# Two graph layers in one kernel: layer 2 with the adjacency as weights, and four smaller moves in layer 1

## The reference

```
h  = relu(layernorm(x))
s  = (h @ W) @ a1 ;  t = (V @ W) @ a2
e  = leaky(s[:, None] + t[None, :], 0.2), where adj > 0, else -9e15
x  = x + elu(softmax(e, axis=1) @ V + h)
h2 = relu(layernorm(x))
x  = x + relu((adj.T @ h2) @ U.T / adj.sum(axis=0)[:, None])
```

## Time and profile before

| | us |
|---|---|
| median of 3 runs (lowest, highest) | 490.03 (489.5, 490.09) |
| the profiled execution | 489.36 |
| its span | 487.5 |
| PE / DVE / ACT / POOL busy | 425.2 / 299.1 / 255.0 / 127.8 |
| weight row copied on ACT (L448), starts | 11.63 |
| last quarter of V landed (issued 5.47, under way 9.13) | 14.6 |
| first adjacency load issued; lands after | 15.26; 7.7 |
| third and fourth adjacency load: issued; land after | 16.5 and 17.0; 16.2 and 20.5 |
| first guard; shifts of group 0 turned (1.87); seeds; first mask | 26.23; 46.71; 49.26; 50.08 |
| closing of group 4: DVE starts at 407.00, h2 scaled at 416.69 + 0.69 | 10.4 |
| one score of 5 blocks on DVE (L738) | 0.86 |
| relu and exp of 5 blocks on ACT: 109.18 (0.77), 110.10 (0.79) | 1.6 |
| DVE step over 256 elements (L875, L878) | 0.40 to 0.42 |
| ACT copy of 500 columns from PSUM; POOL's subtraction (L379) | 0.59; 1.15 |
| clock granted to TensorE, mean share | 0.963 |

### The profile page before, as it was taken

How to read it: one execution, slowest core, us unless ns; L and a number is a source line. 1 busy time by engine, 2 the same in 40 slices (tenths; PEclk the granted TensorE clock), 3 DMA queues, 4 the chain that set the end, 5 groups by cost and what they waited for, 6 DMA issues and landing times.

```text
span 487.5 us, 9207 instructions
## 1 busy us (share of the span) xinstructions
PE 425.2 (87%) x3966; PEld 200.5 (41%) x3966; DVE 299.1 (61%) x401; ACT 255.0 (52%) x306; POOL 127.8 (26%) x118
## 2 busy tenths in 40 slices
PE   0511989799987999998999999999999999999996
PEld 0411344354332544332444333354333436655563
DVE  4799489669999578999469999523443313101011
ACT  1210457575654776776776766877777741100010
POOL 8750058476242702321202223101010001200000
PEclk9975699799999999999999999999999999999999
DMA  9799999999999790000000000000000000000001
GB/s 162 83 107 108 107 102 107 108 107 109 107 102 101 77 99 1 1 2 0 1 1 2 1 1 1 1 1 1 1 1 2 1 1 3 0 12 12 21 19 27
DMA packets 17638, 20.74 MB, mean 43 GB/s; under 512 B 13409, under 2 KB 13473, under 8 KB 17598
## 3 DMA queue, kind: packets, MB, share of 16 engines
q0 software_dynamic: 4752, 16.90, 33.5%
q1 hardware_dynamic: 8606, 2.18, 2.3%
q10 hardware_dynamic: 4240, 1.08, 1.3%
HBM read 69.79 MB, written 1.05 MB: 145 GB/s over the span
## 4 chain that ended last, share of the span: by engine, by line
PE 60%; DVE 23%; issue 9%; ACT 4%; DMA 2%; ACTq 1%; POOL 1%; DVEq 0%; POOLq 0%
PE att L988 16%; DVE junk L692 14%; PE q L972 10%; PE den L991 9%; PE q L1077 7%; DVE arena L738 5%; PE q L1047 3%; PE den L1077 3%; DMA v_sb<-n_L_gnn_entity_embs_dram 2%; PE att L1077 2%; PE z L937 2%; ACT q L529 2%; PE z L952 2%; ACT arena L513 2%; PE z L1093 1%
## 5 line engine op out<-in xcount | busy, mean ns | idle before, releaser
L988 PE MATMUL att<-arena,v_sb 128*64 128x500 f32 (+2 forms) x640 | 151.1, 541 | 5.0 <-ACT arena L517 3.2
L692 DVE CUSTOM_DVE_ANT_0 junk<-adj_sb,t_row 125x2048 uint8<-125x2048 uint8 x66 | 153.5, 2326 | 0.7
L738 DVE SCALAR_TENSOR_TENSOR arena<-arena,b_col,q 128x1000 f32<-128x1000 f32 (+2 forms) x80 | 85.7, 1071 | 89.5 <-PE q L972 89.5
L517 ACT ACTIVATE arena<-arena,t 128x1000 f32<-128x1000 f32 (+2 forms) x80 | 78.6, 982 | 89.0 <-DVE arena L738 88.9
L972 PE MATMUL q<-bi,adj_sb 128*128 128x125 bf16 (+1 forms) x1088 | 90.1, 221 | 14.7 <-ACT q L529 9.8
L991 PE MATMUL den<-arena,ones 128*32 128x250 f32 (+1 forms) x1280 | 94.5, 354 | 0.0
L972 PEld LDWEIGHTS q<-bi,adj_sb 128*128 128x128 fp8e4 x1088 | 64.4, 99 | 72.1 <-issue 42.9
L529 ACT ACTIVATE q<-arena,minus_b 128x1000 f32<-128x1000 f32 (+2 forms) x80 | 76.0, 950 | 7.3 <-PE q L963 1.2
L513 ACT ACTIVATE arena<-q,t_col 128x1000 f32<-128x1000 f32 (+2 forms) x80 | 74.7, 934 | 2.8 <-PE q L972 2.4
L991 PEld LDWEIGHTS den<-arena,ones 128*32 128x32 f32 x1280 | 25.4, 109 | 107.9 <-issue 107.9
L988 PEld LDWEIGHTS att<-arena,v_sb 128*64 128x64 f32 x640 | 32.2, 137 | 22.8 <-ACT arena L517 5.6
(11 more groups left out here) (152 smaller groups left out, 295.6 us busy)
## 6 DMA issues: line engine op xcount, KB each, us to landing
adj_sb<-in_adj_dram POOLq DMA_DIRECT2D x33, 500.0 KB, 28.6
v_sb<-n_L_gnn_entity_embs_dram ACTq DMA_DIRECT2D x4, 256.0 KB, 9.1
x_sb<-in_x_dram SPq DMA_DIRECT2D x1, 928.0 KB
out_dram<-x_sb SPq DMA_DIRECT2D x7, 124.0 KB
x_sb<-in_x_dram SPq DMA_DIRECT2D x1, 125.0 KB
out_dram<-x_sb SPq DMA_DIRECT2D x1, 125.0 KB
buf_a<-in_L_gnn_a_dram ACTq DMA_DIRECT2D x1, 32.0 KB, 3.0
buf_b<-in_L_gnn_U_dram SPq DMA_DIRECT2D x2, 16.0 KB, 6.4
```

Of the source, the lines that this page charges most:

```text
L517: nc.scalar.activation(e_part(n % E_SLOTS, nb), e_part(n % E_SLOTS, nb), ACT.Exp, bias=t02[:, c:c + 1])\
L692: nc.vector.tensor_tensor_reduce(out=junk[0:R, :], in0=adj_bytes[0:R, b, half], in1=t_row[0:R, half], scale=1.0 / ONE, scalar=0.0, op0=ALU ...
L738: nc.vector.scalar_tensor_tensor(out=e_part(n % E_SLOTS, nb), in0=a_part(nb), scalar=b_col[:, c:c + 1], in1=part(q[0], nb), op0=ALU.max, o ...
L988: nc.tensor.matmul(att[h * D:(h + 1) * D, 0:(k1 - k0) * R], v_sb[:, c, :], e[:, k0 * R:k1 * R], start=first, stop=final)
```

## The change

1. **Layer 2** takes the adjacency as weights: for each of the 33 blocks of output rows, 33 matmuls with 129 moving columns (h2 high, h2 low, a column of ones whose sum is the degree). The twelve outputs `OUTS` have three or two blocks, one PSUM bank each. Counts, degrees, the copies of the sums and the products go away. U moves into each closing: PE turns h2 (`turn_h2`, tile 17), ACT copies (`copy_turned`, 18), PE multiplies by a doubled U (`times_u`, 19), ACT makes two copies (`high`, 20). U's rows are scaled to norm 1 and the norm is multiplied back at the end (`u_scale`).
2. **Leaky parts**: DVE takes 12, 6, 12, 12, 20 tiles of the five groups, ACT the others; the tiles 0 and 1 of a group are always DVE's. Either kind may use either `q`; the seeds go.
3. **V** comes by two queues, two quarters each; on SP's they stand before x. Five blocks get their ones before V is weighed, and the adjacency loads no longer wait for x.
4. **The mean of V** stands in front of the tiles, behind six of group 0's eight guards.
5. **Turns in bf16**: the shifts are turned in bf16, and turns of fp32 data are transposes.

```diff
-    ONES_FIRST = 9
+    ONES_FIRST = 5
-    ON_ACT = [c % 2 == 1 for i, c in TILES]
-    FIRST_ON_ACT = ON_ACT.index(True)
-    CHUNKS = [(4 * i, 4 * i + 4) for i in range(7)] + [(28, 29), (29, 33)]
+    ON_DVE = (12, 6, 12, 12, 20)
+    ON_ACT = [c >= 2 and (c - 1) * (ON_DVE[i] - 2) // (NC - 2) == (c - 2) * (ON_DVE[i] - 2) // (NC - 2) for i, c in TILES]
+    OUTS = [(3 * i, 3 * i + 3) for i in range(9)] + [(27, 29), (29, 31), (31, 33)]
+    PART_A = 6
+    STORE = 112
...
-        turn = sb("turn", [P, 8, 32])
+        turn = sb("turn", [P, 8, 32], bf16)
...
+        TURN_H2, COPY_H2, TIMES_U, HIGH = 17, 18, 19, 20
...
+            def load_v(i):
+                chunks = slice(i * NC // PARTS, (i + 1) * NC // PARTS)
+                sp.dma_start(v_sb[:, chunks, :], v_view[:, chunks, :]).then_inc(v_in[i], 16)
+
             sp.dma_start(w_sb, W[:, :]).then_inc(wa_in, 16)
+            load_v(1)
+            load_v(3)
             sp.dma_start(x_sb[:, 0:SHORT, :], x_short).then_inc(x_in, 16)
...
+                sp.wait_ge(fin_done, o + 1)
+                sp.dma_start(to[0:STORE], x_sb[0:STORE, b0:b1, :]).then_inc(out_stored, 16)
+                sp.dma_start(to[STORE:rows], x_sb[STORE:rows, b0:b1, :]).then_inc(out_stored, 16)
...
-            pool.wait_ge(x_in, 32)
             for b in range(ONES_FIRST):
                 load(b)
+            for b in range(ONES_FIRST, 7):
+                set_ones(b)
+                load(b)
...
+            nc.gpsimd.memset(h2[:, :, 2 * D:2 * D + 1], 1.0).then_inc(ones_made, 1)
+            pool.wait_ge(u_bounded, 1)
+            pool.wait_ge(ones_made, 1)
+            nc.gpsimd.tensor_tensor(u_inverse[:, :], u_squares[:, :], minus_half[0:D, 0:1], ALU.pow).then_inc(u_inverted, 1)
...
-            for i in range(PARTS):
+            for i in (0, 2):
                 chunks = slice(i * NC // PARTS, (i + 1) * NC // PARTS)
                 act.dma_start(v_sb[:, chunks, :], v_view[:, chunks, :]).then_inc(v_in[i], 16)
...
-                act.wait_ge(h2_done, i + 1)
-                nc.scalar.activation(h2[0:R, b0:b1, 0:D], buf_a[0:R, 0:b1 - b0, :], ACT.Copy).then_inc(hi_done, 1)
+                act.wait_ge(h2_multiplied, i + 1)
+                nc.scalar.activation(h2[0:R, b0:b1, 0:D], product, ACT.Copy).then_inc(hi_done, 1)
+                nc.scalar.activation(buf_a[0:R, 0:b1 - b0, :], product, ACT.Copy).then_inc(h2_copied, 1)
...
+            for o, (b0, b1) in enumerate(OUTS):
+                rows, nb = rows_of(b0), b1 - b0
+                mine = buf_a[0:rows, o % 2 * 4:o % 2 * 4 + nb, :]
+                dve.wait_ge(gathered, o + 1)
...
+                nc.vector.reciprocal(rdeg[0:rows, 0:nb].unsqueeze(2), sums(o)[:, :, 2 * D:2 * D + 1]).then_inc(rdeg_done, 1)
...
+                nc.vector.tensor_reduce(mine, sums(o)[:, :, 0:2 * D].rearrange("p k (h d) -> p k d h", h=2), AX.X, ALU.add)\
+                    .then_inc(halves_added, 1)
...
+                nc.vector.scalar_tensor_tensor(out=mine, in0=mine, scalar=0.0, in1=rdeg[0:rows, 0:nb].unsqueeze(2).to_broadcast([rows, nb, D]),
+                                               op0=ALU.max, op1=ALU.mult).then_inc(scaled, 1)
...
+                nc.vector.tensor_tensor(mine, mine, u_scale[0:rows, :].unsqueeze(1).to_broadcast([rows, nb, D]), ALU.mult)\
+                    .then_inc(widened, 1)
...
+                nc.vector.tensor_tensor(x_sb[0:rows, b0:b1, :], x_sb[0:rows, b0:b1, :], mine, ALU.add).then_inc(fin_done, 1)
...
-                    pe.wait_ge(a_copied, 1)
-                    pe.wait_ge(bi_made, 1)
+                    pe.wait_ge(guarded, 2 * GROUPS[0][1] - 2)
                 last = nc.tensor.matmul(z[:, 1, :], mean_w, v_sb[:, 8 * k:8 * k + 8, :].rearrange("p c d -> p (c d)"),
...
-                    nc.tensor.matmul(z[0:R, 0, k * P:(k + 1) * P], scratch[:, k * R:(k + 1) * R], ident[:, :], start=True, stop=True)
+                    turn_over(z[0:R, 0, k * P:(k + 1) * P], scratch[:, k * R:(k + 1) * R], P)
...
             rows(0)
+            for k in range(4):
+                mean_v(k)
             turn_shifts(0)
...
+            def gather(o, first, last_one):
...
+                for k in range(b1 - b0):
+                    start = first_row(b0 + k)
+                    for b in range(first, last_one):
+                        rows = rows_of(b)
+                        done = nc.tensor.matmul(out_bank(o)[0:out_rows, k * (2 * D + 1):(k + 1) * (2 * D + 1)],
+                                                adj_sb[0:rows, b, start:start + out_rows], h2[0:rows, b, 0:2 * D + 1],
+                                                start=(b == 0 and k == 0), stop=(b == NB - 1 and k == b1 - b0 - 1))
...
+            late = GROUPS[-1][0]
+            pe.wait_ge(exped, len(TILES))
+            pe.wait_ge(lo_done, NI - 1)
+            pe.wait_ge(ones_made, 1)
+            gather(0, 0, late)
             to_natural(NI - 1)
...
+            for o in (1, 2, 3):
+                gather(o, 0, late)
+            turn_h2(NI - 1)
+            gather(4, 0, late)
+            times_u(NI - 1)
+            gather(5, 0, late)
+            pe.wait_ge(lo_done, NI)
+            for o in range(PART_A):
+                gather(o, late, NB)
+            for o in range(PART_A, len(OUTS)):
+                gather(o, 0, NB)
```

More of the change, by code:

```diff
@@ L542, in _ @@
                         square2(i - 1)
+                    if c == COPY_H2:
+                        copy_turned(i - 1)
                     if c == HIGH:
@@ L563, in _ @@
             copy_att(NI - 1)
[L565 to L570 removed]
             act.wait_ge(weighed, NC * NI)
[L573 removed]
             exp_hp(NI - 1)
             square2(NI - 1)
+            copy_turned(NI - 1)
             high(NI - 1)
[L577 to L583 removed]
         @block.vector
@@ L936, in turn_shifts @@
                     for bank, start, c0, c1 in block_parts(nb, k):
-                        last = nc.tensor.matmul(z[96:P, bank, start:start + c1 - c0], turn[0:R, k, :], ident[0:R, c0:c1],
+                        last = nc.tensor.matmul(z[96:P, bank, start:start + c1 - c0], turn[0:R, k, :], ident16[0:R, c0:c1],
                                                 start=True, stop=True)
@@ L1027, in _ @@
                     to_natural(i - 1)
+                if i >= 1 and c == TURN_H2:
+                    turn_h2(i - 1)
+                if i >= 1 and c == TIMES_U:
+                    times_u(i - 1)
                 if i == 0:
-                    if MEAN_V <= c < MEAN_V + 4:
-                        mean_v(c - MEAN_V)
                     if c == TURN_U:
@@ L1039, in _ @@
                 attend(n, *TILES[n])
-            def count(k):
-                pe.wait_ge(exped, len(TILES))
-                for b in range(NB):
-                    for quarter, n in enumerate(COUNTS[k]):
-                        first = first_row(CHUNKS[n][0])
-                        last = nc.tensor.matmul(count_banks[k][32 * quarter:32 * quarter + 32, 0:width(n)], ones16[0:rows_of(b), :],
-                                                adj_sb[0:rows_of(b), b, first:first + width(n)], start=(b == 0), stop=(b == NB - 1))
-                last.then_inc(counted, 1)
@@ L1064, in gather @@
-            def gather(n):
-                first = first_row(CHUNKS[n][0])
-                if n in (3, 4, 5):
-                    pe.wait_ge(deg_copied, n - 2)
-                if n >= 6:
-                    pe.wait_ge(agg_copied, n - 5)
-                for b in range(NB):
-                    if n == 0 and b == 0:
-                        pe.wait_ge(lo_done, NI - 1)
-                    if n == 0 and b == GROUPS[-1][0]:
-                        pe.wait_ge(lo_done, NI)
-                    rows = rows_of(b)
-                    last = nc.tensor.matmul(gather_banks[n % 6][:, 0:width(n)], h2[0:rows, b, :],
-                                            adj_sb[0:rows, b, first:first + width(n)], start=(b == 0), stop=(b == NB - 1))
-                last.then_inc(gathered, 1)
```

247 lines of the change are left out of this document (122 added, 125 removed).

## The result

The changed kernel takes **483.18 us** (median of 11 runs, 481.83 to 488.35) against 489.36 for the one before (11 runs, 488.64 to 490.24): a ratio of 0.9887, 95% interval 0.9857 to 0.9917. It is faster, by 6 us where 45 were forecast, and lies above the range of 434 to 470. The profiled execution took 482.21, its span is 480.4.

A forecast was written before the change was run, and what follows sets the result against it. PE was taken to bound groups 2 to 4 and layer 2, with waits in groups 0 to 3. Terms -6.5 - 9.9 - 5.1 - 2.7 - 2.2 + 1.0 - 19.9 = -45.3 gave 445 us, range 434 to 470.

The forecast's parts named there:

- The tiles: Groups 0 to 4: new DVE/ACT sharing shrinks waits; terms -9.9, -5.1, -2.7, -2.2 and +1.0 us.
- PE's floors: Groups 1 to 3: PE's time with no wait after the change, put at 59.4, 72.6 and 72.6 us.
- Rival (c): Groups 0 to 3: new sharing moves the wait to ACT, they gain half or nothing; 455 to 465 us, 13%.
- the closing of group 4 hides: Layer 2's beginning: gathers cover the last group's closing chain; if that failed, a wait of 1 to 2 us.
- Group 0: First group's tiles: loses mean of V and seeds, PE and DVE level at 42; 47 us, -9.9.
- Group 4: Last group's tiles: no turn of shifts to save on, h2 turn and U added; +1.0 us.
- Layer 2: Final gather: 1089 matmuls with adjacency as weights, 66.0 us against 85.9, -19.9.
- The open price: Layer 2: cost of the weight load behind each matmul, taken as 57 ns, ends 56.4 and 111.
- (a): Layer 2: load costs more than the matmul, 65 to 84 ns instead of 57; 454 to 474 us, 14%.
- (b): Layer 2: load goes at fp32's rate, 111 ns a pair, 59 us more; 504 us, 9%.
- The start: Before the first mask: V by two queues -4.5 us, seeds and half the turn -2.0; first mask near 43.5.
- rival (d): Start: two queues don't bring V sooner, or x is caught among large transfers; +5 to +10, 450 to 455 us, 7%.

The follow-up runs named there:

- the best kernel: The changed kernel with the old sharing (every odd tile on ACT) and DVE's sums of s at tile 24 instead of 21: 453.41 us, 0.9271.
- the alternation: The changed kernel with the old sharing of the leaky parts back, every odd tile on ACT, 16 and 16: 461.3 us, 0.9444.
- the moved guards: Guards dealt over the first 23 tiles instead of 26, against the 453.4 us kernel with old alternation and sums at tile 24: 463.55 us, 0.9472.

## Why the prediction failed, point by point

**The failed step** is the one called "The tiles", at the sentence "I expect DVE's waits to shrink, not to go", and with it the terms -5.1, -2.7 and -2.2 of groups 1 to 3. These terms left 2, 1.4 and 1.4 us of waits above PE's floors of 59.4, 72.6 and 72.6; measured above the floors are 8.7, 11.5 and 14.6. The step compared each engine's sum with the stage (ACT 66 of 73, DVE 49 of 60) and took the difference as slack. The sums were not far off: ACT has 59.9 in group 2, DVE 49.35 in group 1. What decides is which wait stands ahead of which instruction in an in-order queue, and that I did not write out for the new rule. Had I laid tiles 0 to 5 of a group in a row, relu 2 behind exp 0, relu 3 and the copy of att behind exp 1 were plain to see, with two guards in front. Those first tiles are where the whole price of the sharing sits, some 19 us over the five groups. The floors were also reckoned at full clock; behind the waits it was half.

**Rival (c)** had the same places and the right sign against the forecast, with the wrong mechanism (ACT's load, 2.27 against 2.12) and the wrong size: "gain half or nothing". A sharing that couples engines can lose, and did, 15 us in the kernel before.

**The second oversight** is the late product. In the closing I counted what the product adds on PE and asked whether the closing of group 4 hides; for groups 0 to 3 I followed the closing to `high` but not to who waits behind it: POOL's low half, `weigh_h` behind that, `sum_s` at tile 21. "What is late next" was the question to ask of every tile number moved from 17 to 20. It cost 7.9 to 13.2 us.

**Group 0** was put at 47 with ends of 43 and 54; it took 52.8, and 50.8 in the best kernel. The premise, two engines level at 42, did not hold: DVE is busy 38.3 us there and PE 45.0, at a mean clock of 0.90. What holds group 0 was not taken apart. **Group 4** came out 2.9 above its term. Its pitches at tiles 1 to 3 are 2.56, 3.11 and 3.01 (with the alternation 2.11, 2.37 and 3.01), and at tile 21 the mask waits 0.9 for a relu that stands behind ACT's two copies of `high`.

**Layer 2** held: 66.6 for 66.0. The open price, 57 ns a pair between 56.4 and 111, measured 58.4; the load itself, which I set at 57 from the ratio of fp32 and narrow matmuls, measured 56.7 or less (65 moving columns). Rivals (a) and (b) fall with it. The Trainium skill (TensorE: Matmul & The Clock Gate, LDWEIGHTS) would have had an estimate of 103 ns; the measurement decides against it for fp8 weights. What the Trainium skill says in its section on Fast Weight Load (same page), that the full 128 columns are needed, agrees with the durations (97 ns at 128 columns, 135 at 124). Here that bought nothing, since matmuls of 129 columns hide either load. That the closing of group 4 hides was right as well: 1089 gathers at 58.4 are 63.6 us and PE is busy 66.1 of 66.6.

**The start** held: first mask at 42.22 for 43.5. The two queues with V ahead of x are worth 5.0 of it, -4.5 by the prediction, and rival (d) falls. The Trainium skill (DMA: Bandwidth & Descriptors, Issuing engines are not separate DMA queues) lets a second issuer save issue time only. ACT's issues, 7.17 us for four against 1.47 for two, agree: its table load is 5.7 us sooner, the first adjacency load 4.6 (10.75 for 15.32). V's place ahead of x changed in the same run and was not told apart.

The parts together: with the old alternation and the sums at 24, the change is worth 36 us of the 45 forecast. Of the rest, 8.7 stand in groups 0 to 3 (3.8, 2.3, 0.6 and 2.0 above their terms), so layer 2, the start and group 4 were right within 0.7 each.

What stays open: whether a new sharing without the two DVE tiles at each start, or with the copy of att ahead of exp 1, would gain anything, since none was run; why the late product costs 12.6 us with the new sharing, 8.8 with the old, and nothing seen with 16 DVE tiles by the new rule (DVE's wait for POOL is 2.9 us there, for 9.8 and 6.2); and what group 0 waits for.

## What to carry to other kernels

Before moving work between engines, write down for a few tiles what stands ahead of each instruction in its queue; an engine that is busy 60% can still hold the bound one up if a ready instruction stands behind one that waits for a third engine. Look first at the few tiles where one group's ending meets the next one's start: both the sharing and the moved guards lost most of their time there, in part by a copy out of PSUM that came late. When a closing or any chain gets longer, follow it to its last consumer, and move that consumer's place in the order too: here one number, 21 to 24, gave 7.9 us. A filler that is ahead of a short urgent step isn't bad by itself: where it fills a wait that is there anyway, moving it behind puts it ahead of the next urgent step.

## What was not expected of the hardware

An fp8 weight load of 124 columns binds at 56.7 ns a pair at most, where little else fills the time, half of the 111 ns of fp32, though its duration in the trace is 135 ns; durations of loads overlap and do not add up to a rate. A matmul of 129 fp16 columns costs 58.4 to 58.5 ns whether its load lasts 97 or 135; by the 2.6 ns over the columns of the 124-column row it should be 56.4. And at the start of group 3 two waits of PE, 1.39 and 2.08 us, were followed by some 3 us at the 1.2 GHz level, where the kernel before has 1.00 in its rows of groups 1 to 4.
